# attention_2 in steps of two units, the context's scores made ahead of the loop, three banks for the transposes

## The reference, cut to what matters

```python
l = layer_norm(latents, ln2_g, ln2_b)
q = l @ Wq
kv_in = jnp.concatenate([x, l], axis=1)      # 32 context tokens + 512 tokens
k, v = jnp.split(kv_in @ Wkv, 2, axis=-1)
w = softmax(einsum('bhqd,bhkd->bhqk', q * scale, k * scale))
out = einsum('bhqk,bhkd->bhqd', w, v)        # then @ Wo
```

## Time and profile before

| | us |
|---|---|
| median of 3 runs | 2162.71 (2161.41 to 2165.06) |
| the profiled execution, its own time | 2162.47 |
| its span | 2160.7 |
| TensorE busy in the span | 1918.4 (89%) |
| VectorE busy | 1218.6 (56%) |
| ScalarE busy | 926.0 (43%) |
| GpSimd busy | 805.5 (37%) |

### The profile page before, as it was taken

The page is one execution under the profiler, slowest core; times in us unless marked ns, Lnnn a source line. Parts: engine busy times, 40 slices in busy tenths (PEclk is TensorE's granted clock), DMA queues, the critical chain, the costliest instruction groups (busy, mean ns, idle before and its releaser), DMA issues. The chain is left out here.

```text
span 2160.7 us, 32154 instructions
## 1 busy us (share of the span) xinstructions
PE 1918.4 (89%) x11205; PEld 1237.5 (57%) x11205; DVE 1218.6 (56%) x3077; ACT 926.0 (43%) x2062; POOL 805.5 (37%) x960
## 2 busy tenths in 40 slices
PE   5697899898969899898969989989897998979899
PEld 4465465565746556555655646646574565656555
DVE  6568365453866546464576636636375564554554
ACT  1154455264532455254543435617353551642221
POOL 3336265452520146354351116535252554530000
PEclk9788899898979999998989989989898999999999
DMA  5300000002030000002002000000200000030030
GB/s 199 125 1 1 1 1 1 1 2 79 1 124 1 5 1 1 1 1 69 12 21 104 1 5 2 1 1 2 79 1 1 1 1 1 1 118 1 6 117 6
DMA packets 33743, 59.08 MB, mean 27 GB/s; under 512 B 6448, under 2 KB 11184, under 8 KB 32944
## 3 DMA queue, kind: packets, MB, share of 16 engines
q1 hardware_dynamic: 33584, 57.03, 7.5%
HBM read 53.86 MB, written 3.16 MB: 26 GB/s over the span
## 5 line engine op out<-in xcount | busy, mean ns | idle before, releaser
L1246 POOL TENSOR_TENSOR rows<-rows,rinv 128x512 f32<-128x512 f32 x256 | 260.7, 1039 | 315.5 <-DVE rinv L1431 315.5
L1426 DVE TENSOR_REDUCE nmax<-psum 128x2 f32<-128x1088 f32 x128 | 165.2, 1290 | 125.6 <-PE psum L1296 125.6
L1387 ACT ACTIVATE rows<-psum,nmax 128x544 f32<-128x544 f32 x256 | 180.6, 710 | 49.6 <-DVE nmax L1426 49.4
L2021 ACT ACTIVATE region_b<-psum 128x512 f32<-128x512 f32 x132 | 78.8, 597 | 255.2 <-PE psum L1966 255.1
L2062 DVE TENSOR_TENSOR region_b<-region_b,psum 128x512 f32<-128x512 f32 x128 | 87.9, 686 | 161.0 <-PE psum L1990 154.0
L1290 PE MATMUL psum<-region_a,region_b 64*128 64x256 f32 x1024 | 162.0, 408 | 9.7 <-ACT rows L1387 6.0
L1306 PE MATMUL psum<-weights,rows 128*128 128x128 f32 x1024 | 163.3, 282 | 8.2 <-ACT turned L1394 4.7
L1990 PEld LDWEIGHTS psum<-region_c,region_b 128*128 128x128 f32 x1024 | 133.7, 192 | 47.6 <-issue 27.9
L1306 PEld LDWEIGHTS psum<-weights,rows 128*128 128x128 f32 x1024 | 115.6, 149 | 60.3 <-issue 60.3
L1324 PE MATMUL psum<-turned,region_a 128*64 128x256 f32 x1024 | 137.9, 391 | 3.8 <-DVE turned L1437 3.5
L1394 ACT ACTIVATE turned<-psum 128x512 f32<-128x512 f32 x128 | 76.7, 599 | 146.4 <-PE psum L1306 146.4
(11 more groups left out here) (468 smaller groups left out, 3816.1 us busy)
## 6 DMA issues: line engine op xcount, KB each, us to landing
region_a<-w_centred SPq DMA_DIRECT2D x32, 258.0 KB, 5.3
region_a<-in_w SPq DMA_DIRECT2D x32, 256.0 KB, 4.5
region_a<-in_eg SPq DMA_DIRECT2D x32, 256.0 KB, 5.8
region_a<-in_eu SPq DMA_DIRECT2D x32, 256.0 KB, 6.0
region_c<-in_weights SPq DMA_DIRECT2D x32, 256.0 KB, 6.8
weights<-in_weights SPq DMA_DIRECT2D x1, 3489.0 KB, 15.7
w_centred<-region_a SPq DMA_DIRECT2D x8, 258.0 KB, 2.2
region_a<-in_w SPq DMA_DIRECT2D x1, 2048.0 KB, 12.5
```

What stands on the lines that cost most here:

```text
L1246: nc.gpsimd.tensor_tensor(row, row, rinv[:, 2 * u + j:2 * u + j + 1].broadcast_to([P, S]), ALU.mult).then_inc(done, 1)
L1387: nc.scalar.activation(heads_of(u, j), scores_of(u, j), ACT.Exp, bias=nmax[:, 2 * u + j:2 * u + j + 1], accum_out=psum_of[:, 2 * u + j:2 * ...
L1426: nc.vector.tensor_reduce(nmax[:, 2 * u:2 * u + 2], both_scores(u), AX.X, ALU.max, negate=True).then_inc(s.mx, 1)
```

## The change

All of it lies in `attention_2`; the other stages stay as they are. There are now 16 steps of two units each (two of the four query tiles of a pair).

- The context's scores of all 32 units are made in the head, 32 products of 64 columns into banks 4 to 7. ScalarE copies them into `aot` in four pieces, and VectorE takes their negated maxima into `red` (four reductions of 512).
- In the loop the maximum is made in two operations: a reduction over the 1024 main scores of both heads, then a minimum (`ALU.min`, since the values are negated) with the context's part. The second waits for the first.
- Per step GpSimd adds the maxima to the step's 128 context scores, ScalarE takes their exp, VectorE sums them (`ctx_sums`), and the sum of main and context parts is added ahead of each reciprocal. GpSimd then multiplies the 128 context weights at the end of the step.
- Main scores use banks 0 to 3, the transposes go round banks 4, 5 and 6. The probability rows have four buffers (the fourth in `xn` and `xnt`) instead of three.
- TensorE's step is: scores of two units, a whole values product of the step before the last, [context product], sixteen transposes of the step before, and in every second step four context transposes. VectorE copies the four context transposes out at once.
- The values of the tokens (`vtok`) are made after the scores of units 0 and 1, through four banks, evicted in turn by ScalarE and VectorE.

The core of the diff, with lines that only rename things left out:

```diff
+            steps = units // 2
+            last_rows = (xn[:, :, :].rearrange("p t d -> p (t d)"), xnt[:, :])
+
+            def s_bank(u, j):
+                return bank(2 * (u % 2) + j)
...
+                return bank(2 * (u % 2), 2).rearrange("p (j k) -> p j k", j=2)
+
+            def row(u, j):
+                return rows2[:, 1024 * (u % 4) + 512 * j:1024 * (u % 4) + 512 * (j + 1)] if u % 4 < 3 else last_rows[j]
+
+            def ctx_rows(n):
+                return aot[:, n // 2, 4 * K * (n % 2):4 * K * (n % 2 + 1)]
+
+            def turned_to(n, i):
+                return turned2[:, 2 * (n % 2) + i % 2, :, P * (i // 2):P * (i // 2 + 1)]
+
+            def place(n, i):
+
+                return 4 * n + i + n // 2
+
+            def ctx_place(p):
+                return 9 * p + 8
+
+            def turn_bank(at_place):
+                return bank(4 + at_place % 3)
+
+            def wait_copied(pe, at_place):
+                p, r = at_place // 9, at_place % 9
+                done = 2 * (2 * p + r // 4) + r % 4 // 2 + 1
+                if r == 8:
+                    pe.wait_ge(s.cc, p + 1)
+                elif r % 2 == 0:
+                    pe.wait_ge(s.ca, done)
+                else:
+                    pe.wait_ge(s.cb, done)
...
+                    pool.wait_ge(s.cx_copied, T)
...
+                    for n in range(steps):
+                        four = ctx_rows(n).rearrange("p (h k) -> p h k", k=K)
+                        pool.wait_ge(s.mx, 2 * n + 2)
+                        nc.gpsimd.tensor_tensor(four, four, over(nmax[:, 4 * n:4 * n + 4], 2, [P, 4, K]),
+                                                ALU.add).then_inc(s.shifted, 1)
+                        normalise(2 * n)
+                        normalise(2 * n + 1)
+                        nc.gpsimd.tensor_tensor(four, four, over(rinv[:, 4 * n:4 * n + 4], 2, [P, 4, K]),
+                                                ALU.mult).then_inc(s.pc, 1)
...
-                    for n in range(10):
-                        k, half = n // 2, n % 2
-                        rows = P if k < 4 else 2 * K
-                        tokens = kvt[:, P * k:P * k + rows]
...
-                        nc.tensor.matmul(bank(4 + n % 2)[0:rows, :], tokens,
-                                         wkv2[:, H2 * HD2 + 512 * half:H2 * HD2 + 512 * (half + 1)],
-                                         start=True, stop=True).then_inc(s.pq, 1)
...
+                    for t in range(T):
+                        for p in range(PAIRS):
+                            mm = nc.tensor.matmul(bank(4 + t)[:, 2 * K * p:2 * K * (p + 1)], qtt[:, p, P * t:P * (t + 1)],
+                                                  kctx[:, 2 * p:2 * p + 2, :], start=True, stop=True)
+                        mm.then_inc(s.cx, 1)
...
+                                mm = nc.tensor.matmul(s_bank(u, j)[:, 256 * half:256 * (half + 1)],
+                                                      qtt[lo:lo + 64, p, P * t:P * (t + 1)],
+                                                      ktt[lo:lo + 64, p, 256 * half:256 * (half + 1)], start=True, stop=True)
+                        mm.then_inc(s.s, 1)
+
+                    def turn(n):
+                        for i in range(4):
+                            u, j = 2 * n + i // 2, i % 2
+                            pe.wait_ge(s.pn, 2 * u + j + 1)
+                            if place(n, i) >= 3:
+                                wait_copied(pe, place(n, i) - 3)
+                            for k in range(T):
+                                mm = nc.tensor.transpose(turn_bank(place(n, i))[:, P * k:P * (k + 1)],
+                                                         row(u, j)[:, P * k:P * (k + 1)], ident[:, :])
+                            mm.then_inc(s.t, 1)
...
+                    def turn_ctx(p):
+                        pe.wait_ge(s.pc, 2 * (p + 1))
+                        wait_copied(pe, ctx_place(p) - 3)
+                        for t in range(T):
+                            mm = nc.tensor.transpose(turn_bank(ctx_place(p))[0:2 * K, P * t:P * (t + 1)],
+                                                     aot[:, p, 2 * K * t:2 * K * (t + 1)], ident[:, :])
+                        mm.then_inc(s.t, 1)
+
+                    def values(n):
+                        p, half = n // 2, n % 2
+                        pe.wait_ge(s.ca, 2 * (n + 1))
+                        pe.wait_ge(s.cb, 2 * (n + 1))
+                        if p >= 1 and half == 0:
+                            pe.wait_ge(s.on, p)
...
-                    for step in range(units + 5):
-                        v = step - 4
-                        if step >= 8 and step % 4 == 0:
-                            context(step // T - 2)
-                        if step < units:
-                            scores(step)
-                        if LAG <= step < units + LAG:
-                            turn(step - LAG, 0)
-                            turn_ctx(step - LAG)
-                        if 0 <= v < units:
-                            values(v // T, v % T // 2, v % 2 == 0)
-                        if LAG <= step < units + LAG:
-                            turn(step - LAG, 1)
+                    scores(0)
+                    scores(1)
+                    for n in range(10):
+                        k, half = n // 2, n % 2
+                        rows = P if k < 4 else 2 * K
+                        if n < 4:
+                            pe.wait_ge(s.cx_copied, n + 1)
+                        else:
+                            pe.wait_ge(s.v_act if n % 2 == 0 else s.v_dve, n // 2 - 1)
+                        nc.tensor.matmul(v_bank(n)[0:rows, :], kvt[:, P * k:P * k + rows],
+                                         wkv2[:, H2 * HD2 + 512 * half:H2 * HD2 + 512 * (half + 1)],
+                                         start=True, stop=True).then_inc(s.v, 1)
+
+                    for n in range(1, steps + 2):
+                        if n < steps:
+                            scores(2 * n)
+                            scores(2 * n + 1)
+                        if n == 1:
+                            pe.wait_ge(s.v_act, 5)
+                            pe.wait_ge(s.v_dve, 5)
+                        if n >= 2:
+                            values(n - 2)
+                            if n % 2 == 1:
+                                context(n // 2 - 1)
+                        if n <= steps:
+                            turn(n - 1)
+                            if n % 2 == 0:
+                                turn_ctx(n // 2 - 1)
...
+                    for t in range(T):
+                        act.wait_ge(s.cx, t + 1)
+                        nc.scalar.activation(aot[:, :, 2 * K * t:2 * K * (t + 1)], bank(4 + t).rearrange("p (a k) -> p a k", k=2 * K),
+                                             ACT.Copy).then_inc(s.cx_copied, 1)
...
+                    def ctx_exps(n):
+                        act.wait_ge(s.shifted, n + 1)
+                        nc.scalar.activation(ctx_rows(n), ctx_rows(n), ACT.Exp).then_inc(s.cx_exp, 1)
...
-                    for step in range(units + 5):
-                        if step >= 8 and step % 4 == 0:
-                            copy_heads(step // T - 2)
-                        if LAG <= step < units + LAG:
-                            copy_first(step - LAG)
-                        if step < units:
-                            exps(step, 0)
-                            exps(step, 1)
+                    def evict(dst, src):
+                        return nc.scalar.activation(dst, src, ACT.Copy)
+
+                    exps(0)
+                    for n in range(0, 10, 2):
+                        act.wait_ge(s.v, n + 1)
+                        if n == 8:
+                            act.wait_ge(s.zero, 1)
+                        v_evict(evict, n).then_inc(s.v_act, 1)
+                    ctx_exps(0)
+                    exps(1)
+                    for n in range(1, steps + 3):
+                        if n >= 4 and n % 2 == 0:
+                            copy_heads(n // 2 - 2)
+                        if n < steps:
+                            exps(2 * n)
+                            ctx_exps(n)
+                        if n <= steps:
+                            copy_turned(n - 1, 0)
+                        if n < steps:
+                            exps(2 * n + 1)
+                        if n <= steps:
+                            copy_turned(n - 1, 2)
...
+                    for t in range(T):
+                        dve.wait_ge(s.cx_copied, t + 1)
+                        nc.vector.tensor_reduce(red[:, H2 * t:H2 * (t + 1)].rearrange("p (a j) -> p a j", j=2),
+                                                aot[:, :, 2 * K * t:2 * K * (t + 1)].rearrange("p a (j k) -> p a j k", k=K),
+                                                AX.X, ALU.max, negate=True).then_inc(s.cx_max, 1)
+                    dve.wait_ge(s.cx_max, T)
```

(79 more changed lines are left out.)

108 lines of the change are left out of this document (22 added, 86 removed).

## The result

The changed kernel takes **2192.68 us** (median of 4 runs, 2192.05 to 2193.55) beside 2162.06 for the kernel before on the same chip: ratio 1.0147 [1.0132, 1.0162], 30.6 us slower. The forecast was 2173, slower by 10. The direction held, and the time lies inside the wide range, 2134 to 2197, but outside the forecast's own, 2158 to 2186: the loss is three times the one forecast. Spans: 2190.2 after, 2160.7 before; mean granted clock 0.926 and 0.935.

What follows compares the result with a forecast made beforehand. TensorE's queue bounded the kernel before; afterwards VectorE, held by GpSimd, sets a 14.7 us pair against 15.19. A call takes 141.2 us against 139.6; +1.5 and +1.0 for clock make +10 us in all: 2173 us, range 2134 to 2197.

Steps and rivals of the forecast that it cites:

- the granted clock of the head: Clock allowance, placed in the first loop steps (step 1) of each call: 1.0 us a call added, 0 to 3 possible.
- the 16.2 us: Loop steps 1 and 2 after the head: 8.0 and 8.2 us, with waits on VectorE's evictions, context sum and ScalarE's copy.
- 7.4: Head: 64 context records on TensorE at the pace of the output projection (64 in 7.41 us).
- records slower than 0.12 us each: Failure sign in the head: the forecast fails if context products run slower than 0.12 us a record.
- Head without the clock: Whole call with its new head, before any clock term: 141.2 us against 139.6.
- The pair: Steady loop, two steps: period 14.7 us after the change against 15.19 before.
- holding: Loop: GpSimd passes hold VectorE's two-SBUF-input minima and additions, 2.4 us a pair, of which 1.3 lengthens it.
- the hand-over: Loop, before `ctx_sums`: minimum to GpSimd's addition to ScalarE's exp to VectorE's sum; VectorE idle 0.97 us, twice a pair.
- the wait of TensorE for ScalarE's copy: Loop, every second step: TensorE waits 1.5 us for the first transposed rows' copy, queued behind the context's exp.
- Rival 1: Loop: small operations slip past GpSimd's passes; pair 13.4 us, -7.1 us a call, 2134 us, faster; chance 0.22.
- Rival 2: Longer hand-over, hops 0.10 to 0.15 us, half clock through head and drain (+3): 2197 us, slower; chance 0.20.
- Rival 3: Loop: TensorE stays the limit at 12.9 us a pair, about -11 us a call, 2119 us; chance 0.08.

Runs made afterwards that it cites:

- e5_add_only: The changed kernel, 64-column products kept, with only the loop's addition made a one-SBUF-input reduction (the minimum keeps two inputs): 2183.23 us, ratio 1.0097.
- e1_wide: The changed kernel with the head's context products made 128 columns wide instead of 64 (seven of eight per query tile): 2169.19 us, ratio 1.0037.

## Why the prediction was right or wrong

**The step that failed is the granted clock of the head**: "I add 1.0 us a call, 0 to 3 being possible". Widening the products gave back 5.9 us a call by the medians; against the calls whose head kept its clock the loss is 6.9, and within one execution 6.5. The forecast looked for the fall in the first loop steps, where it stood before. It is there too, in the second step, but inside the 16.2 us that the first two steps were to take without it. Step 2 takes 8.1 with about 1.6 of clock in it; how much of this a step at full clock would spend on other waits, no run shows. In the head, the forecast took the 64 context records at the pace of the output projection, "7.4", without asking whether a run of 64-column records keeps the clock that 128-column ones keep; its last paragraph names the case, records slower than 0.12 us each, but gives it neither a price nor a chance. They took 0.18 to 0.22. The 13.7 or 17.1 us at half clock then also made the first scores slower (3.5 to 3.8 for 2.0) and, in the first call, the values' products (9.5 from the first of them to the next scores, for 8.9), and the other engines had too little to do beside it to hide the loss.

**Head without the clock**: right. With the products 128 wide, the two calls whose head kept its clock take 142.4 us on average, 1.3 more than before; the forecast's sum without a clock term gave +1.6. From the first to the third unit's scores the forecast had 10.7 + 0.35 = 11.05; it is 10.87 in the wide run.

**The pair**: right, 14.66 for 14.7, and for the forecast's reasons: holding (1.09 us a pair measured, 1.3 forecast), the hand-over (0.85 idle, with 0.085 of early start lost, for 0.97), the wait of TensorE for ScalarE's copy in every second step (1.13, and 0.19 for VectorE's copy behind it, for 1.5). The 0.04 us between two dependent operations of VectorE, for which the forecast had no row, are 0.03 to 0.04 here (minimum behind maximum, addition behind sum).

**Rival 1**, no holding: its premise is wrong for the change as made, since operations of two columns are held to the end of a pass, as those of 4 and 32 columns in the earlier trace rows are (the rule of the Trainium skill that the prediction cites, "SBUF — State Buffer", section Who interferes with whom, held in these runs too); its price, 13.4, was nearly that of the kernel in which nothing is held, 13.57. **Rival 2** put the loss at a longer hand-over and a clock at half "through head and drain (+3)"; its total, 2197, is near the measured one, but its main term is not there: hops are 0.03 to 0.08, the pair is 14.66 and not 15.3. Only its clock term was on the right track, and it was less than half the size. **Rival 3** is the bound that the run without the hand-over reaches.

Per call, then: 8.2 us measured, 6.9 of it the clock in the head and 1.3 all the rest, where the forecast had 1.0 and 1.6.

What stays open: why the stretch of 64-column products lost its clock in 15 traced calls of 16 and kept it in one, and why the 128-column one lost it for 3.4 us in 7 of 16. Only the width was varied; mixing the narrow products with other work was not tried.

## What to carry to other kernels

When work is gathered into a stretch of its own, look at what that stretch is made of: a run of narrow matmuls can lower the granted clock for itself and for what follows, even if TensorE never stops; widening them, with columns that nobody reads, cost nothing here and gave back 1.1%. On VectorE beside a busy GpSimd, count SBUF operands and not elements: a two-operand step on two columns lasted up to 0.98 us where it takes 0.16 unheld, and with its operands side by side, as a reduction, 0.16. Cost held time by where it lies on the cycle; its sum says little. Here freeing the minima alone brought 1.06 us of the 1.09 a pair, and freeing the additions alone 0.49.

## What was not expected of the hardware

- 64 fp32 matmul records of 128x64 take 7.33 us at full clock (fourth call of e5_add_only), as long as 64 of 128x128 (7.33, e1_wide). Between these two widths the number of columns sets no time here, but it goes with the clock, which was at half for 13.7 or 17.1 us in 15 of 16 calls with the narrow ones and for at most 3.4 us with the wide ones.
- An estimate: a change of TensorE between kinds of products costs about 0.21 us, from the pair of 13.15 us without the hand-over less the forecast's 11.67 us for its products and transposes, over seven changes.
